# Reordering the end of the third layer, where its norm hands tiles to the last layer, in a four-layer graph network

## The reference

```
# third layer: its result is the norm of a sum
neigh = segment_sum(h[dst] @ W_neigh.T + b_neigh, src) / deg
out   = relu(h @ W_self.T + b_self + neigh)
s     = h + out
x     = x + (s - mean(s)) * rsqrt(var(s) + 1e-5) * gamma + beta
# fourth layer: two graph convolutions, with self loops
h = relu(layernorm(x))
h = relu(gcn(h, W1, b1));  x = x + gcn(h, W2, b2)
# gcn: segment_sum((h @ W)[src] * dis[src] * dis[dst], dst) + b, dis = deg ** -0.5
```

## Time and profile before

| | |
|---|---|
| median of 3 runs | 668.75 us (668.55 to 669.43) |
| the profiled execution's own time | 668.7 us |
| its span, first to last instruction | 666.8 us |
| TensorE (PE) busy | 647.4 us, 97% |
| VectorE (DVE) busy | 375.8 us, 56% |
| ScalarE (ACT) busy | 304.3 us, 46% |
| GpSimd (POOL) busy | 42.8 us, 6% |
| granted TensorE clock | 0.999 |

### The profile page before, as it was taken

How to read it: one execution, slowest core, us unless ns; L and a number is a source line. 1 busy time by engine, 2 the same in 40 slices (tenths; PEclk the granted TensorE clock), 3 DMA queues, 4 the chain that set the end, 5 groups by cost and what they waited for, 6 DMA issues and landing times. The chain is left out here.

```text
span 666.8 us, 11295 instructions
## 1 busy us (share of the span) xinstructions
PE 647.4 (97%) x3199; PEld 525.6 (79%) x3200; DVE 375.8 (56%) x870; ACT 304.3 (46%) x629; POOL 42.8 (6%) x45
## 2 busy tenths in 40 slices
PE   6989999999999999999999999999998899999997
PEld 4336777778888888888888888888886898899886
DVE  6998998855664433324344567554999731440222
ACT  4886777644422134752214341213676863464210
POOL 2000000000000000000000000000356070000000
PEclk9999999999999999999999999999999999999999
DMA  6311111142460002100001020000200000000102
GB/s 221 100 21 21 31 33 36 31 141 64 146 131 0 0 1 79 63 1 0 0 0 65 15 64 0 0 0 2 79 0 1 0 2 1 1 0 1 47 17 94
DMA packets 26272, 25.17 MB, mean 38 GB/s; under 512 B 14076, under 2 KB 17972, under 8 KB 26232
## 3 DMA queue, kind: packets, MB, share of 16 engines
q1 hardware_dynamic: 24952, 22.12, 11.5%
q10 hardware_dynamic: 1280, 2.56, 1.1%
HBM read 17.20 MB, written 4.20 MB: 32 GB/s over the span
## 5 line engine op out<-in xcount | busy, mean ns | idle before, releaser
L1619 PE MATMUL ps<-p_hi,cstage 128*128 128x512 f32 x400 | 156.4, 391 | 0.0
L1619 PE MATMUL ps<-p_lo,cstage 128*128 128x512 f32 x400 | 155.7, 389 | 0.0
L1525 PE MATMUL ps<-w_hi,hT_hi 128*128 128x512 f32 x320 | 128.9, 403 | 0.6 <-issue 0.3
L1525 PE MATMUL ps<-w_hi,hT_lo 128*128 128x512 f32 x320 | 125.1, 391 | 0.0
L1525 PE MATMUL ps<-w_lo,hT_hi 128*128 128x512 f32 x320 | 124.8, 390 | 0.0
L1619 PEld LDWEIGHTS ps<-p_hi,cstage 128*128 128x128 f32 x400 | 75.1, 188 | 16.5 <-issue 0.4
L1619 PEld LDWEIGHTS ps<-p_lo,cstage 128*128 128x128 f32 x400 | 75.1, 188 | 15.4
L1030 DVE TENSOR_SCALAR src_hot<-iota,nodeT 128x640 bf16<-128x640 f16 x210 | 70.8, 380 | 4.2 <-issue 2.0
L1504 PE MATMUL ps<-src_hot,dst_hot 128*128 128x320 bf16 x420 | 67.6, 306 | 5.3 <-DVE src_hot L1030 2.8
L1525 PEld LDWEIGHTS ps<-w_hi,hT_lo 128*128 128x128 f32 x320 | 60.0, 188 | 13.1
L1525 PEld LDWEIGHTS ps<-w_hi,hT_hi 128*128 128x128 f32 x320 | 60.1, 188 | 12.7 <-issue 1.1
(11 more groups left out here) (152 smaller groups left out, 904.2 us busy)
## 6 DMA issues: line engine op xcount, KB each, us to landing
x<-in_x ACTq DMA_DIRECT2D x1, 2304.0 KB
out_x<-x SPq DMA_DIRECT2D x9, 256.0 KB
wstage<-in_L_gnn_W SPq DMA_DIRECT2D x2, 1024.0 KB, 5.4
swap<-count SPq DMA_DIRECT2D x2, 800.0 KB, 8.7
count<-swap SPq DMA_DIRECT2D x2, 800.0 KB, 8.4
wstage<-in_L_gnn_W_l SPq DMA_DIRECT2D x2, 512.0 KB, 4.2
w_own<-in_L_gnn_W_r SPq DMA_DIRECT2D x1, 1024.0 KB, 11.0
vec<-in_L_gnn_b SPq DMA_DIRECT2D x4, 256.0 KB, 7.7
```

Of the source, the lines that this page charges most:

```text
L1525: last = nc.tensor.matmul(ps[:, bank, :], a[:, r, k, :], w[:, slot, k, :], start=n == 0, stop=n == len(pairs) - 1)
L1619: last = nc.tensor.matmul(ps[:, AGG + r, :], cstage[:, part, k, :], p_[:, k, :], start=n == 1, stop=n == 2 * len(parts) * NT)
```

## The change

It has four parts. (1) VectorE's order of calls from `receive(8, 0)` to the end of tile 9 is another one: the statistics and scales of tiles 4 to 6 come ahead of `features_lo(0)`, and the closing of tiles 8 and 9 is spread between and behind the later `features_lo`. (2) Tile 7's scaled sum is added to `x` by VectorE (`add_sum(7, 1)`) instead of by ScalarE (`scale_centred`) and GpSimd (`add_scaled`). (3) The scales and shifts are made one column, that is one tile, at a time, with one tensor input and a per-partition scalar. (4) ScalarE's list follows the new order.

```diff
 # GpSimd, small counts (in the branch for large counts add_scaled(NT - 3) is left out)
-                        with pool.Fori(1, NT - 1) as i:
+                        with pool.Fori(1, NT - 2) as i:
                             add_beta(i)
                             add_scaled(i - 1)
+                        add_beta(NT - 2)
                         add_beta(NT - 1)
 # ScalarE, last_layers
                 features_hi(1)
-                scale_centred(NT - 3, 1)
-                root_of_sum(NT - 2, 0)
+                deviation(v, 6)
                 make_features(4)
                 make_features(5)
                 features_hi(2)
                 features_hi(3)
                 spread_(0, 2, 5)
-                deviation(v, 6)
                 features_hi(4)
                 features_hi(5)
+                spread_(0, 5, 6)
                 deviation(v, 7)
-                spread_(0, 5, 7)
+                spread_(0, 6, 7)
                 make_features(6)
                 make_features(7)
                 features_hi(6)
                 features_hi(7)
+                root_of_sum(NT - 2, 0)
                 spread_(0, 7, 11)
 # VectorE, feature_scales
-                    nc.vector.tensor_tensor(scale3[:, a:b], rstd[:, a:b], dis[:, a:b], ALU.mult).then_inc(scale3_done, b - a)
-                    dve.wait_ge(scale3_done, b)
-                    nc.vector.scalar_tensor_tensor(shift3[:, a:b].unsqueeze(2), mv[:, a:b, 0:1], -1.0,
-                                                   scale3[:, a:b].unsqueeze(2), ALU.mult,
-                                                   ALU.mult).then_inc(shift3_done, b - a)
+                    for i in range(a, b):
+                        nc.vector.tensor_scalar(scale3[:, i:i + 1], rstd[:, i:i + 1], dis[:, i:i + 1], None,
+                                                ALU.mult).then_inc(scale3_done, 1)
+                    for i in range(a, b):
+                        dve.wait_ge(scale3_done, i + 1)
+                        nc.vector.tensor_scalar(shift3[:, i:i + 1], mv[:, i, 0:1], scale3[:, i:i + 1], -1.0, ALU.mult,
+                                                ALU.mult).then_inc(shift3_done, 1)
 # VectorE, the order
                     receive(8, 0)
                     centre_sum(7, 1)
+                    new_statistics(6)
+                    aggregate_statistics(6)
+                    feature_scales(4, 6)
                     add_relus(8, 0)
                     features_lo(0)
-                    feature_scales(4, 6)
-                    sum_statistics_1(8, 0)
-                    sum_statistics_2(8, 0)
+                    add_sum(7, 1)
                     features_lo(1)
-                    new_statistics(6)
-                    aggregate_statistics(6)
                     receive(9, 1)
                     features_lo(2)
                     new_statistics(7)
                     aggregate_statistics(7)
                     features_lo(3)
+                    sum_statistics_1(8, 0)
                     feature_scales(6, 8)
+                    features_lo(4)
+                    sum_statistics_2(8, 0)
                     add_relus(9, 1)
-                    features_lo(4)
+                    features_lo(5)
+                    sum_statistics_1(9, 1)
+                    features_lo(6)
+                    sum_statistics_2(9, 1)
                     centre_sum(8, 0)
-                    features_lo(5)
+                    features_lo(7)
                     add_sum(8, 0)
-                    features_lo(6)
-                    sum_statistics_1(9, 1)
-                    sum_statistics_2(9, 1)
-                    features_lo(7)
                     new_statistics(8)
                     aggregate_statistics(8)
                     centre_sum(9, 1)
```

More of the change, by code:

```diff
@@ L519, in _ @@
                     general_columns(NT - 1)
-                    add_scaled(NT - 3)
                     add_beta(NT - 1)
```

## The result

The changed kernel takes 663.66 us (median of 6 runs, 662.99 to 665.04) against 668.69 for the one before (6 runs, 667.35 to 669.43): a ratio of 0.9926, 95% interval 0.9916 to 0.9936, that is 4.3 to 5.6 us less. The forecast was 664.8, 3.9 less. The profiled execution took 663.0, with a span of 661.2 us.

The account below looks back on a forecast made before the run. TensorE, busy in 97% of the span, bounds the kernel; its stops before steps 1 to 4 can be won. Step 7 at 523.7 instead of 527.6 gives 668.75 - 3.9 = 664.8 us, range 663.4 to 666.6.

Parts of the forecast that it names:

- The bound and the path: TensorE's stops around layer 3's steps 0 to 4: about 5.5 us at most to win; the end moves with them.
- Columns aren't held: VectorE's one-column scales run free beside GpSimd additions, like the reciprocal; 0.77 us a call for two tiles.
- The first rival: One-column scales are held by GpSimd's additions as well: 2.9 us less, 665.8; chance 0.13.
- `p_lo` 0 at 512.6: VectorE before step 0: `p_lo` 0 starts at 512.6, taken between 513.0 and 512.1; step 0 about 0.9 later.
- doesn't reach TensorE, but for one place: Scales of tiles 0 to 3: gain covered by aggregation matmuls except at ScalarE's late staging of last counts, 0.1 to 0.2.
- The low end of 512.1: Start of `p_lo` 0 on VectorE with 0.6 us gained ahead and GpSimd done in time.
- `p_lo` 0 to `p_lo` 4: VectorE's list between these two operations takes 6.03 us, with nothing held since GpSimd has nothing left.
- One stop at step 4 of 0.4: TensorE in layer 3's steps: 1 to 3 don't stop, step 4 stops 0.4 us, none behind it to step 7.
- ScalarE: ScalarE's reordered list keeps up; thinnest margin 0.4 us, at `deviation(7)` before the scales of 6 and 7.
- The second rival: ScalarE becomes the late one, steps 4 to 7 about 1.5 later: 2.4 us less, 666.3; chance 0.10.
- the third: The stop only moves: tile 8 or 9, closed after `p_lo` 7, stops step 16: 668.5; chance 0.03.
- the fourth: Slower: VectorE stands at tile 6's statistics for a late `x` 6, ahead of `p_lo` 0: 670.6; chance 0.04.

Follow-up runs that it names:

- the tighter order: Changed kernel with bounds asserted on list lengths, VectorE's centring of tile 7 and `add_relus(8)` moved behind `p_lo` 0: 663.90 us, again 663.33.
- the experiment with columns from tile 4 on: Changed kernel with bounds asserted on list lengths, scales of tiles 0 to 3 in the old two-tile, two-tensor-input form: 666.10 us, ratio 0.9952.

## Why the prediction was right, and where a term was off

*The bound and the path.* Right. Step 4 was the last stop, and all behind it moved with it: 4.66 us at step 4, 4.62 at the end. The bound itself, 5.5 us, was too low: the tighter order wins 5.74 and 5.76. There TensorE starts step 0 0.61 us earlier from zero (45.43 against 46.04), where I counted 0.2, and needs 5.14 us less from step 0 to step 7, where I counted 5.3.

*Columns aren't held.* Right, taken from the free reciprocal: 0.33 for two at 492.01 beside GpSimd. A call takes 0.70 (509.33 to 510.03, GpSimd's last addition ending within it) and 0.68 with GpSimd idle (515.87 to 516.55), where I had 0.77. The first rival (a hold on them too) is out. The Trainium skill's Vector Engine (DVE) Microarchitecture Reference ("5.1 Performance modes — why throughput varies by op and dtype") enables a two-port mode for tensor_scalar on SBUF operands. At one element per partition this trace shows no hold beside GpSimd (0.33 for two); which mode the engine ran it does not show.

*`p_lo` 0 at 512.6.* This is the term that was off. From zero that is 46.1; measured is 45.49. It was a middle between two ends: 513.0 (46.5) if nothing is gained ahead, and 512.1 (45.6) with 0.6 gained at `receive(8)` and GpSimd done in time. Both ends have their kernel: with tiles 0 to 3 in the old form `p_lo` 0 starts at 46.52, with the columns everywhere at 45.49. So the columns of tiles 0 to 3 are worth 1.03 us at `p_lo` 0, and the sentence that their gain "doesn't reach TensorE, but for one place" (0.1 to 0.2 us) failed. That one place gave nothing: TensorE starts its last aggregation matmul 0.29 us earlier (45.18 against 45.47 from zero), and then stands 0.71 us for `p_lo` 0. I followed VectorE's own gain (`receive(8)` 0.64 us earlier by 41.72 and 41.08, as said) and kept the end of GpSimd's last addition at 512.5 (46.0 from zero). But its additions came 1.56 us earlier, by way of ScalarE as the experiment with columns from tile 4 on shows, and the last ended at 44.49, before `add_relus(8)` began. With 45.49 in its place and all other terms as forecast, step 7 comes at 45.49 + 11.07 = 56.56 against 61.13 before: 4.6, the measured value.

Two errors in that term partly cancelled, which is luck. From its start `add_relus(8)` was given 1.26 us up to `p_lo` 0 (511.74 to 513.0), and it took 0.60. The centring of tile 7 was given 0.97, and it took 1.45 (506.95 to 508.40), since it meets GpSimd's addition earlier. The low end of 512.1 isn't worked out either: the forecast's own terms with 0.6 gained and nothing to hold `add_relus(8)` give 508.20 - 0.6 + 0.87 + 0.97 + 0.93 + 0.77 + 0.60 = 511.74, 45.26 from zero.

*`p_lo` 0 to `p_lo` 4.* 6.03 forecast, 5.92 measured (510.63 to 516.55), most of the difference being the scales, 0.68 where I had 0.77. One stop at step 4 of 0.4 was forecast; step 4 came 5.95 after step 0, 0.3 later than at TensorE's own pace (5.63). Steps 1 to 3 didn't stop.

*ScalarE.* Right to a tenth: features of 4 from 0.60 before `p_lo` 0's start, deviation of tile 7 done 0.4 before the scales of 6 and 7 began. The second rival did not occur, nor the third (no stop behind step 4), nor the fourth (VectorE did not idle before tile 6's statistics). A late `x` of tile 6 was not tried by itself.

*Between trace and times.* 4.62 us by the trace's stretch and 5.03 by the medians agree within the interval (4.3 to 5.6).

## What to carry to other kernels

When GpSimd and VectorE share a stage, count GpSimd's lateness as a quantity of its own: an operation held far ahead of the critical stop, under cover of TensorE's matmuls, can still shift GpSimd's next ones onto the operations in front of that stop. Give the time beside a GpSimd addition to one-input work (statistics, reciprocals, scales by column) and put the two-input operations behind it. And two edits that each win most of the same stop are not added up: 3.27 and 3.07 made 4.61 here.

## What the runs showed of the hardware that was not expected

That an operation on two elements per partition can take 1.25 to 1.28 us beside a GpSimd addition (0.16 alone), and that the hold goes by the second SBUF tensor and not by the width: a one-element operation is held as well (two in 1.33 to 1.36), statistics over 512 elements are not (0.68 at 508.40, beside GpSimd). An operation with one tensor in PSUM and one in SBUF isn't held: `receive(8)` at 506.22 has its normal 0.75 us beside GpSimd's additions, which run without a gap from 505.37 to 509.63. The taking in turn goes both ways: GpSimd's own addition grows from 1.29 to 1.75 us where a VectorE operation that was held goes first (501.11 in the kernel with columns from tile 4 on).
